# Four tiles placed per dense unit, slots units two units sooner and closed up, in a mixture-of-experts block

## The reference

```
xn = _layernorm(x)
Q = relu(rope_rotate(xn @ W_Q)); H = tanh(Q + hh_b)
s = swapaxes(group_norm_rows(H, gn_weight, gn_bias), -2, -1).reshape(B, T, C)
sc = sigmoid(xn @ Wr.T + br)                  # 32 experts in 8 groups
idx = top 6 experts of the top 4 groups;  w = 2.5 * sc[idx] / sum(sc[idx])
moe = sum over experts e of gate[:, e] * (square(relu(xn @ W1[e].T)) @ W2[e].T)
shared = square(relu(xn @ Ws1.T)) @ Ws2.T
out = x + s * silu(shared + moe)
```

## Time and profile before

| | |
|---|---|
| three runs | 384.57, 388.2, 391.12 us; median 388.2 |
| profiled execution | 388.77 us, of which the span on the core 387.0 |
| busy share of the span | TensorE 84%, VectorE 71%, ScalarE 64%, GpSimd 53% |
| mean granted TensorE clock | 0.954 of full speed |
| unit 12's rounding, first slots unit's, last slots unit's, last unit's | 88.6, 119.2, 280.2, 378.2 us |

### The profile page before, as it was taken

One profiled execution on the slowest core, in us unless ns is written; L12 is line 12 of the kernel. 1 busy time (PEld: TensorE's weight loads), 2 busy tenths in 40 slices (PEclk: granted clock), 3 DMA queues, 4 the chain that ended last, 5 costly groups with the idle time before them and its releaser, 6 DMA issues.

```text
span 387.0 us, 8250 instructions
## 1 busy us (share of the span) xinstructions
PE 324.5 (84%) x2725; PEld 237.4 (61%) x2725; DVE 274.1 (71%) x655; ACT 247.6 (64%) x411; POOL 206.4 (53%) x220
## 2 busy tenths in 40 slices
PE   0576975999978879879798788989999999999992
PEld 0344734667767758658677576767867666666661
DVE  4788889988962646955879543674656698786876
ACT  4878889556575575657767558769764654444443
POOL 1967977756772453424645346440025656675750
PEclk9996889899996999989999899999999999999999
DMA  7951160356851553643546445373559467676651
GB/s 260 394 175 55 49 205 2 102 162 194 263 185 37 160 157 115 186 136 127 175 132 194 141 131 174 121 210 92 167 144 354 152 179 207 183 181 177 182 147 68
DMA packets 37626, 62.65 MB, mean 162 GB/s; under 512 B 5042, under 2 KB 25938, under 8 KB 37586
## 3 DMA queue, kind: packets, MB, share of 16 engines
q1 hardware_dynamic: 30914, 43.90, 35.8%
q0 software_dynamic: 6672, 18.23, 16.7%
HBM read 47.18 MB, written 14.93 MB: 160 GB/s over the span
## 4 chain that ended last, share of the span: by engine, by line
PE 57%; DVE 13%; issue 10%; ACT 6%; DVEq 6%; ACTq 3%; POOL 2%; DMA 1%; another core or an unknown queue 0%
PE hp L946 6%; PE hp L944 6%; PE hp L945 6%; PE dp L1003 5%; PE dp L1002 5%; PE dp L1000 5%; PE rot L908 4%; PE rot L961 3%; PE hp L931 2%; PE hp L933 2%; PE rot L959 2%; PE hp L932 2%; PE rot L960 2%; DVEq L1303 2%; ACTq L691 2%
## 5 line engine op out<-in xcount | busy, mean ns | idle before, releaser
L606 POOL DMA_INDIRECT xgt<-xtab,ids x85 | 87.7, 1032 | 82.2 <-PE rot L908 59.6
L687 ACT ACTIVATE hf<-hf 128x512 f32<-128x512 f32 (+2 forms) x96 | 55.8, 581 | 66.6 <-DVE hf L1257 33.6
L616 POOL DMA_INDIRECT wst<-ytab,slot x54 | 55.9, 1035 | 58.8 <-DMA ytab<-wst 27.4
L1000 PE MATMUL dp<-wt,hhi 128*128 128x256 f16 x238 | 65.7, 276 | 2.8 <-DVE hlo L1264 1.4
L1002 PE MATMUL dp<-wt,hlo 128*128 128x256 f16 x238 | 65.6, 276 | 2.7 <-issue 2.7
L1003 PE MATMUL dp<-wt,hhi 128*128 128x256 f16 x238 | 65.5, 275 | 2.4 <-issue 2.3
L692 ACT ACTIVATE hhi<-hf 128x512 f16<-128x512 f32 (+2 forms) x96 | 55.9, 582 | 6.8
L1257 DVE SCALAR_TENSOR_TENSOR hf<-hp,gate_bc 128x512 f32<-128x512 f32 (+1 forms) x64 | 39.7, 621 | 28.2 <-PE hp L946 21.9
L944 PE MATMUL hp<-xh,wt 128*128 128x512 f16 (+2 forms) x148 | 57.8, 390 | 1.6 <-issue 1.3
L945 PE MATMUL hp<-xh,wt 128*128 128x512 f16 (+2 forms) x148 | 57.8, 390 | 0.0
L946 PE MATMUL hp<-xh,wt 128*128 128x512 f16 (+2 forms) x148 | 57.6, 389 | 0.0
(11 more groups left out here) (174 smaller groups left out, 694.8 us busy)
## 6 DMA issues: line engine op xcount, KB each, us to landing
ytab<-wst SPq DMA_DIRECT2D x42, 256.0 KB
wst<-in_wts SPq DMA_DIRECT2D x17, 512.0 KB, 5.0
gate_bc<-gtab SPq DMA_DIRECT2D x32, 256.0 KB
gate_bc<-gtab SPq DMA_DIRECT2D x32, 192.0 KB
xs<-in_x SPq DMA_DIRECT2D x4, 512.0 KB, 6.1
xgt<-in_x SPq DMA_DIRECT2D x4, 512.0 KB
out<-xgt SPq DMA_DIRECT2D x16, 128.0 KB
xtab<-xn SPq DMA_DIRECT2D x3, 512.0 KB, 3.1
```

What stands on the lines that cost most here:

```text
L606: nc.gpsimd.indirect_dma_start(xg[:, a % XRING, :, :].rearrange("p h d -> p (h d)"), None, xtab, bass.IndirectOffsetOnAxis(ids[:, a:a + 1] ...
L616: nc.gpsimd.indirect_dma_start(yk[:, n % KRING, :], None, ytab, bass.IndirectOffsetOnAxis(slot[:, n // K, n % K:n % K + 1], 0))\
L687: nc.scalar.activation(hf[:, k % HP, 0:width(k)], hf[:, k % HP, 0:width(k)], ACT.Square, scale=W_SCALE ** (-0.5 if gated else -1.0))
L1000: nc.tensor.matmul(o, hhi[:, k % HRING, hcols], hi, start=(e == 0 and q % 2 == 0), stop=False, skip_group_check=True)
```

## The change

Four routed tiles are placed per dense unit, in units 8, 9 and 10; `PLACED` becomes 11. The first one-hot has only the 85 columns that exist, and its scaling by the row number is done by ScalarE (`rows_at`) in place. `LEAD` goes from 12 to 10. No dense units stand between the last four slots units, so two more follow them, and the last slots unit leaves its bank one unit after its first layer, not two. There are six places for slot results and six for gathered ones. The gates of block 1 get their root on GpSimd behind the twelfth gather, and are turned in the branch's bank at the head of unit 26, slots unit 5. ScalarE's weight steps lose their delay by one unit (`high_w(k)` throughout).

```diff
-YRING = 3
-KRING = 12
+YRING = 6
+KRING = 6
-LEAD = 12
+LEAD = 10
-        if g % 3:
+        if g % 3 and g < GROUPS - 4:
-        one_a = hots[:, 0]
+        one_a = hots[:, 0, :, 0:TILES]
+        GATES_PAIR = 3
+        GATES_AT = Q_AT(GATES_PAIR)
-        ADD_AT = LAST + 6
+        ADD_AT = LAST + 5
-        PLACED = EARLY + (NR + 1) // 2
+        PLACED = EARLY + -(-NR // J)
+        placed_by = lambda k: range(J * (k - EARLY), min(NR, J * (k - EARLY + 1)))
-        low_by_dve = lambda k: k >= PLACED
+        low_by_dve = lambda k: k >= PLACED - 1
+        left_at = lambda i: i + (1 if i == LAST else 2)
-            W_LOADS = {EARLY: 10, EARLY + 1: 11, EARLY + 2: 12, EARLY + 3: 13, PLACED: 14, PLACED + 1: 15, PLACED + 2: 16}
+            W_LOADS = {EARLY: (10,), EARLY + 1: (11,), EARLY + 2: (12, 13), PLACED: (14,), PLACED + 1: (15,), PLACED + 2: (16,)}
...
             for a in range(TILES):
+                if a == XRING + J:
+                    for b in range(1, len(BLOCKS)):
+                        gate_root(b)
...
+            def rows_at(i):
+                act.wait_ge(tile_ready, i + 1)
+                nc.scalar.activation(one_a[:, i % OHRING], one_a[:, i % OHRING], ACT.Copy,
+                                     scale=row_id[:, ROUTED[i]:ROUTED[i] + 1]).then_inc(row_ready, 1)
             for k in range(EARLY, END):
+                if k < PLACED:
+                    for i in placed_by(k):
+                        rows_at(i)
...
-                if k < WRING + POOL_STEPS:
+                if k < WSTEPS:
                     high_w(k)
-                elif k - 1 < WSTEPS and k > WRING + POOL_STEPS:
-                    high_w(k - 1)
-                if k == PLACED - 1:
+                if k == GATES_AT:
                     for b in range(1, len(BLOCKS)):
                         copy_gates(b)
...
             def turn_gates(b):
                 pe.wait_ge(groot_ready, b + 1)
                 if b > 0:
-                    pe.wait_ge(eoff_ready, 1)
-                    pe.wait_ge(gt_ready, b)
+                    pe.wait_ge(hpre_ready, GATES_PAIR)
...
             def queries(p):
+                if p == GATES_PAIR:
+                    pe.wait_ge(gt_ready, len(BLOCKS))
...
                 if EARLY < k <= PLACED:
-                    place(range(2 * (k - EARLY - 1), min(NR, 2 * (k - EARLY))))
-                if k == PLACED - 1:
+                    place(placed_by(k - 1))
+                if k == GATES_AT:
                     for b in range(1, len(BLOCKS)):
                         turn_gates(b)
...
-                dve.drain()
-                nc.vector.tensor_scalar(one_a[:, s], one_a[:, s], row_id[:, ROUTED[i]:ROUTED[i] + 1], None, ALU.mult)\
-                  .then_inc(one_ready, 1)
...
                 for s in range(POOL_STEPS, WSTEPS):
-                    if k == PLACED + ((s - POOL_STEPS) // 2 if s < WRING + POOL_STEPS else s - POOL_STEPS - 3):
+                    if k == max(s, PLACED + (s - POOL_STEPS) // 2):
                         low_w(s)
```

More of the change, by code:

```diff
@@ L408, in wait_y @@
                 engine.wait_ge(y_out, v + 1 - y_act_before(v + 1))
+        left_at = lambda i: i + (1 if i == LAST else 2)
+        leaving = lambda k: [i for i in (k - 2, k - 1) if i in leaves and UNITS[i][0] == "slots" and left_at(i) == k]
         uses = []
@@ L414, in build @@
                 uses.append(("turn", k + 1, 1))
-            if k - 2 in leaves and UNITS[k - 2][0] == "slots":
-                uses.append(("leave", k - 2, 0))
+            uses += [("leave", i, 0) for i in leaving(k) if i != LAST]
             if k + 2 in leaves and UNITS[k + 2][0] == "slots":
                 uses.append(("turn", k + 2, 0))
-            if k - 2 in leaves and UNITS[k - 2][0] == "slots" and len(leaves[k - 2]) > 1:
-                uses.append(("leave", k - 2, 1))
+            uses += [("leave", i, h) for i in leaving(k) for h in range(i != LAST, len(leaves[i]))]
         use_no = {use: n for n, use in enumerate(uses)}
@@ L511, in _ @@
                     load_gate(dense_no[k] + GRING)
[L512 to L515, removed]
+                for s in W_LOADS.get(k, ()):
+                    load_w(s)
+                if k == GATES_AT + 1:
+                    for b in range(1, len(BLOCKS)):
+                        store_gates(b)
                     sp.wait_ge(gt_stored, 16 * len(BLOCKS))
-                if k - 2 in leaves and UNITS[k - 2][0] == "slots":
-                    store_y(k - 2)
+                for i in leaving(k):
+                    store_y(i)
                 for j in finishing(k - 2):
@@ L596, in _ @@
             low_h(EARLY)
-            for b in range(1, len(BLOCKS)):
-                gate_root(b)
-            for k in range(EARLY + 1, PLACED):
+            for k in range(EARLY + 1, PLACED - 1):
                 low_h(k)
@@ L1071, in _ @@
                     second_shared(k - 2)
-                if before == "slots":
-                    second_slots(k - 2, 0)
+                for i in leaving(k):
+                    if i != LAST:
+                        second_slots(i, 0)
                 if k + 2 < NU and UNITS[k + 2][0] == "slots":
                     turn_slots(k + 2, 0)
-                if before == "slots" and len(leaves[k - 2]) > 1:
-                    second_slots(k - 2, 1)
+                for i in leaving(k):
+                    for h in range(i != LAST, len(leaves[i])):
+                        second_slots(i, h)
                 for p in pairs_at(k, Q_AT):
@@ L1376, in _ @@
                     relu(k)
-                if k - 2 in leaves and UNITS[k - 2][0] == "slots":
-                    leave_slots(k - 2, 0)
+                for i in leaving(k):
+                    if i != LAST:
+                        leave_slots(i, 0)
                 if k - 1 < NU and low_by_dve(k - 1):
                     low(k - 1)
-                if k - 2 in leaves and UNITS[k - 2][0] == "slots" and len(leaves[k - 2]) > 1 and not exit_by_act(k - 2, 1):
-                    leave_slots(k - 2, 1)
+                for i in leaving(k):
+                    for h in range(i != LAST, len(leaves[i])):
+                        if not exit_by_act(i, h):
+                            leave_slots(i, h)
                 for s in range(POOL_STEPS, WSTEPS):
-                    if k == PLACED + ((s - POOL_STEPS) // 2 if s < WRING + POOL_STEPS else s - POOL_STEPS - 3):
+                    if k == max(s, PLACED + (s - POOL_STEPS) // 2):
                         low_w(s)
```

48 lines of the change are left out of this document (25 added, 23 removed).

## The result

The changed kernel takes 399.9 us in the median of four runs (399.2 to 400.5), the kernel before 389.7 beside it (384.6 to 392.0): ratio 1.035, with a 95% interval of 1.026 to 1.044. It is slower. The forecast was 391.4 us with a range of 382 to 398.

A forecast was written before the change was run, and what follows sets the result against it. Every stage but the slots stage was taken as close to TensorE's own work. The terms summed to +3.2 us on a 388.8 us profiled run, 392.0, less 0.6 to the median: 391.4 us, range 382 to 398.

The forecast's parts named there:

- The placement: Placing four tiles per unit: VectorE and TensorE work shrinks, so the stage ends sooner by 7.5 us (6.5 to 9.5).
- T: Start of VectorE's first clipping after the token numbers: 91.15 us before the change, forecast 83.6.
- The lead: Dense units before the first slots unit: ScalarE and VectorE wait on each other's weight steps, losing 5.2 us (3.5 to 6.5).
- Gates of the second block: Head of slots unit 5: TensorE's gate transposes wait for the third bias step, costing 2.5 us (0 to 5.5).
- the third rival: Gates' waits cost 7.2 us, giving 396.1, if the bias step ends over 5 us after TensorE reaches slots unit 5; chance 0.17.
- The roots among the gathers: Second block's 13 GpSimd gate instructions move behind the twelfth gather: costed at nothing, since later gathers are wanted 20 us later.
- Stops of TensorE's issue: The long stop from 111.8 to 117.6 us falls on other instructions, perhaps into a wait: -1.5 us (-4 to +1).
- Last slots units and tail: End of the kernel: last slots units -4.4, four more dense units in the tail +10.4, final adds and closing steps -1.5 us.
- the sum: All terms over the whole kernel: -7.5 + 5.2 + 2.5 - 4.4 + 10.4 - 1.5 - 1.5 = +3.2 us.

The follow-up runs named there:

- e1: Changed kernel with the second block's gates turned in unit 11 and their GpSimd roots early; 356.51 us beside 348.07 for the kernel before, without stops.
- e9: e1's kernel with ScalarE's weight steps 12 to 16 one unit sooner and the gates stored at unit 18; 349.22 us, ratio 1.002 to the kernel before, without stops.
- e12: Kernel before with 128 more already-met waits early in TensorE's list; 349.80 us beside 348.22, without stops.
- e13: Changed kernel as it is, on a chip without stops; 364.91 us beside 348.47 for the kernel before.
- e14: Changed kernel with the roots of the second block's gates early, behind the low half of unit 8; 363.5 us beside 364.9 for the changed kernel, without stops.
- e15: e14's kernel with the gates' transposes moved from the head of slots unit 5 to its end, before the third pair's queries; 359.72 us beside 363.5, without stops.
- e2: Changed kernel with ScalarE's weight steps 12 to 16 one unit sooner; 364.43 us, without stops.
- e3: Kernel before with no dense units between the last four slots units; 351.35 us beside 348.07, without stops.
- e8: Kernel before as it is, on a chip with stops; 389.47 us.

## Why the prediction was wrong

**The placement** was right: T at 83.96, forecast 83.6. By its own terms the working gives 84.0 (the end of the placement at 82.2 and 1.8 us behind it), nearer still. The matmuls with 85 columns stand 0.12 us apart instead of 0.17, so their time followed the moving columns: 6.4 us for the 54, where the forecast took 7.5. What the forecast made of the Trainium skill's sentence on lines of 16 bytes (SBUF — State Buffer, § Door 1: The DMA port swizzle), that the weight load with its stride would have kept them as long as they were, is not borne out here: the stride is the same and the spacing fell.

**The lead** was right: the first slots weights may be loaded at 108.6, forecast 108.3, with the idle times before the weight steps that were named. Mending it gave 7.3 us (e1 to e9, on chips without stops), against a term of 5.2; 5.6 of them lie ahead of the first slots rounding.

**Gates of the second block** is the step that failed: "Between 0 and 5.5 us, I take 2.5", on the ground that "part of that is lost anyway, since the branch's next queries wait for the same step at the end of the same unit". They hardly wait. In the trace of before the queries start at 159.00, just behind that step's end at 158.94, but with only 0.55 us of idle time ahead of them, which the trace puts down to issue:

```profile
159.00 0.28 PE L1018 MATMUL bp<-wqhi,xh 128*128 128x256 f16 x1 [0.55 <-issue]
```

Without stops there is none: in e12 and e1 the step ends over 1 us before the queries come, and TensorE has no idle time there. So at most 0.55 us was to be deducted from the 5.5, and the second wait, for ScalarE's copy behind a whole unit's work, came on top. The two units took 5.7 us more in the trace after, and 6.8 in e13 against e1; the kernel lost 7.0 us by it (e14 against e1). That is the third rival, priced at 7.2 and given 0.17: its mechanism was right and its price near, its chance was too low. Its condition was too strict, though: the third bias step ends 3.9 us after TensorE stands at that unit (at 152.3), not over 5, and both waits came all the same, 4.1 and 1.9 us. e14 and e15 show that the place alone, head or end of the unit, is worth 3.8 of it.

**The roots among the gathers**, "I cost this at nothing": right for the changed kernel without stops (0 by the traces, 1.4 by the medians), but not because the gathers are wanted late. The cover was the lead's own wait; with that gone 6.7 us of waits stood bare (e2). With stops one more stop stands there. That the roots bring it about is not shown, only that it is missing without them.

**Stops of TensorE's issue**, -1.5 forecast. The stop of the lead did leave it (3.5 of the 5.5 us up to the first slots rounding), but another came in slots unit 2 (+4.5), so +1.0.

**Last slots units and tail**, -4.4 + 10.4 - 1.5 = 4.5. In this trace they are -6.1 + 9.5 + 0.3 = 3.7, and 2.5 more from slots unit 17 to 18, a piece that the sum had not counted: 6.2. The forecast took the length of the dense units as all that crosses the line; e3 measured 3.3 us for what the terms put at -0.7. Without stops the tail alone is 12.1 us longer (106.37 in e13, 94.29 in e12), where the forecast had 10.4.

Against the sum of +3.2 this makes +3.2 for the gates, +2.5 for the stops, +1.7 for the end and +0.1 for the rest (T and lead +0.3, other pieces of the stage -0.2): the measured 10.7. On a chip without stops the steps from the changed kernel to the mended one add up: roots early -1.4, transposes behind the unit -3.8, then into the lead -3.2, weight steps ahead with the store late -7.3, end open -1.9: from 364.9 to 347.3 us. They come from three jobs, in which the kernel before had 348.1 to 348.5.

## What to carry to other kernels

Before taking a wait as "lost anyway", look for it in the trace of before: if the instruction that is said to wait shows little or no idle time, nearly the whole price is new, and an in-order engine pays it for everything queued behind. Put such a wait straight ahead of the first instruction that needs the same thing. A slack that covers a moved step may itself be the loss that the next edit removes, so try the edits of one stage together as well as alone; and when units are moved across a boundary, count the instructions on both sides instead of multiplying the length of a unit.

## What the runs showed of the hardware

On some chips the same program ran in 348 us, on others in 387 to 390, and 32 us of the difference lie in the slots stage (3.7 more just ahead of it and 3.8 in the tail, by the traces of before and of e12). On the latter TensorE stops there about every 500 records, for 2 to 5 us, with 0.7 us between single instructions, and its granted clock falls to 0.95 in the mean; on the former the traces kept show no such stop. Up to the end of the lead both kinds agree within 1 us (ScalarE's rounding of unit 12 at 88.65 us in e3 and 88.28 in e8, of unit 17 at 105.91 and 105.33). The stops stay with the same work when the list is shifted by 64 records. Which resource is behind them, and whether they come with the chip or with its state at the time, no run here tells.
